# Two mixture-of-experts stages: expert slots padded to 128 rows in place of 256

## What is computed

```python
logits = einsum('tc,ec->te', x_flat, router_w)
probs = softmax(logits);  top_w, top_idx = top_k(probs, 2)
h = relu(einsum('tc,efc->tef', x_flat, w1) + b1)      # 8 experts, F = 1024
y = einsum('tef,ecf->tec', h, w2) + b2
out = sum over the 2 chosen experts of y * top_w      # layer 0
```

## Time and profile before

| | us |
|---|---|
| median of 3 runs (lowest, highest) | 1844.99 (1844.53, 1845.87) |
| the profiled execution | 1844.98 |
| its span, first to last instruction | 1843.3 |
| TensorE busy | 1593.0 (86%) |
| DVE, ACT, POOL busy | 1115.1, 853.1, 705.1 |
| mean granted TensorE clock | 0.922 |

### The profile page before, as it was taken

How to read it: one execution, slowest core, us unless ns; L and a number is a source line. 1 busy time by engine, 2 the same in 40 slices (tenths; PEclk the granted TensorE clock), 3 DMA queues, 4 the chain that set the end, 5 groups by cost and what they waited for, 6 DMA issues and landing times. The chain is left out here.

```text
span 1843.3 us, 38924 instructions
## 1 busy us (share of the span) xinstructions
PE 1593.0 (86%) x12460; PEld 1169.2 (63%) x12461; DVE 1115.1 (60%) x1945; ACT 853.1 (46%) x1518; POOL 705.1 (38%) x517
## 2 busy tenths in 40 slices
PE   4799798898897669999999996799988689999997
PEld 1433434434336658888888883577767568888886
DVE  4677687677687844555554441788876834444443
ACT  1664764755653425555554441376664322222221
POOL 2400401202200015555555442477771046555564
PEclk9999899899896589999999997699996789999999
DMA  4321311320414554555553222300005353333333
GB/s 132 100 79 46 114 55 36 114 68 23 138 35 168 187 206 92 137 137 137 137 137 69 46 41 38 92 25 17 8 24 180 106 149 59 59 62 60 57 60 44
DMA packets 104311, 159.85 MB, mean 87 GB/s; under 512 B 10810, under 2 KB 69998, under 8 KB 104110
## 3 DMA queue, kind: packets, MB, share of 16 engines
q1 hardware_dynamic: 73007, 117.52, 19.6%
q0 software_dynamic: 29952, 40.91, 12.6%
q10 hardware_dynamic: 1279, 0.46, 0.1%
HBM read 91.49 MB, written 67.37 MB: 86 GB/s over the span
## 5 line engine op out<-in xcount | busy, mean ns | idle before, releaser
L1249 PE MATMUL e_ph<-e_zTt,weights_a 128*128 128x256 f16 x3744 | 425.4, 274 | 29.3 <-issue 27.2
L1249 PEld LDWEIGHTS e_ph<-e_zTt,weights_a 128*128 x3744 | 360.9, 98 | 93.5 <-issue 49.8
L1203 POOL DMA_INDIRECT e_zt<-token_parts,slot_token x156 | 163.6, 1049 | 209.2 <-issue 198.4
L1382 DVE TENSOR_TENSOR e_hl<-e_h,e_hh 128x512 f16<-128x512 f32 x156 | 104.5, 691 | 228.4 <-ACT e_hh L1348 228.4
L1334 ACT ACTIVATE e_h<-e_ph,e_b 128x256 f32<-128x256 f32 x312 | 130.6, 470 | 232.8 <-PE e_ph L1249 155.8
L1213 POOL DMA_INDIRECT token_rows<-e_ysb,slot_token x78 | 148.2, 1901 | 206.9 <-DVE e_ysb L1399 192.5
L1263 PE MATMUL e_pyt<-weights_b,e_hh 128*128 x1248 | 210.7, 273 | 0.7 <-DVE e_ysb L1399 0.7
L647 ACT ACTIVATE probs<-lower_banks,shift 128x1024 f32<-128x1024 f32 x128 | 137.6, 1110 | 119.4 <-PE lower_banks L507 114.4
L1213 POOL DMA_INDIRECT out_dram<-e_ysb,slot_token x78 | 124.4, 1595 | 131.4 <-DVE e_ysb L1403 107.8
L1263 PE MATMUL e_pyt<-weights_b,e_hl 128*128 x624 | 170.2, 273 | 0.0
L1373 DVE SCALAR_TENSOR_TENSOR e_g<-e_ph,e_h 128x512 f32<-128x512 f32 x78 | 54.0, 692 | 174.1 <-PE e_ph L1249 174.1
(11 more groups left out here) (231 smaller groups left out, 2952.5 us busy)
## 6 DMA issues: line engine op xcount, KB each, us to landing
weight_parts<-w_split SPq DMA_DIRECT2D x32, 512.0 KB, 3.3
weights_a<-weight_parts SPq DMA_DIRECT2D x16, 1024.0 KB, 7.4
x_sb<-in_u SPq DMA_DIRECT2D x24, 512.0 KB, 5.1
weight_parts<-x_sb SPq DMA_DIRECT2D x24, 512.0 KB, 3.4
w_raw<-in_w1T SPq DMA_DIRECT2D x16, 512.0 KB, 4.4
w_raw<-in_w2T SPq DMA_DIRECT2D x16, 512.0 KB, 4.7
weights_b<-weight_parts SPq DMA_DIRECT2D x8, 1024.0 KB, 9.6
token_parts<-x_sb SPq DMA_DIRECT2D x8, 1024.0 KB, 5.3
```

The source lines that it names most:

```text
L1203: pool.indirect_dma_start(zt[:, i % 2, c, :], None, g.zrows, at).then_inc(ld[i % 2], 16)
L1249: last = pe.matmul(ph[:, q, f, :], up_w(wp, e, k, 2 * q + f), zTs[:, s, 2 * zp + k, :], start=(n == 0), stop=(n == 5))
L1382: dve.tensor_tensor(hl[:, s, 2 * q:2 * q + 2, :], src[:, q % 2], hh[:, s, 2 * q:2 * q + 2, :], ALU.subtract).then_inc(lo_done, 1)
```

## The change

A block of 128 slots is now the unit to which an expert's slots are padded. `BLOCKS` = 71 in place of 78. `PAIRS` = 28 tiles take two blocks of one expert, then 15 tiles take one block; `NT` = 43. An expert with an odd number of blocks has its last block among the single tiles. The slot numbering gets the steps for this: the ranks from `limit` on are moved `away` to the single tiles.

A single tile has the same number of matmuls in `up`, over 128 columns, and half of `turn` and `down`. It uses two banks of `ph`, by the tile's parity, with four groups of features in a bank where a double tile has two; `py` also goes by parity. In layer 0 a half of `up` is now four activations of 128 columns. Casts, subtractions and the gate product stay 512 columns wide, with one (layer 1) or two (layer 0) of each per single tile. Queues and their order stay; each engine's loop is split into one over double and one over single tiles, with the tiles between written out.

```diff
 C = 2
-NT = (2 * B * S + E * (C * P - 1)) // (C * P)
+BLOCKS = (2 * B * S + E * (P - 1)) // P
+PAIRS = (2 * B * S // P - E) // C
+NT = PAIRS + BLOCKS - C * PAIRS
...
-            step(dve.tensor_scalar(cnti[:], ptot[:, 0:E], float(C * P - 1), None, ALU.add))
-            step(dve.tensor_scalar(cntj[:], cnti[:], (C * P).bit_length() - 1, None, ALU.logical_shift_right))
-            step(dve.tensor_copy(cnt[:], cntj[:]))
-            step(dve.tensor_tensor_scan(cumt[:], g.ones[:, 0:E], cnt[:], 0.0, ALU.mult, ALU.add))
-            step(dve.tensor_tensor(base[:], cumt[:], cnt[:], ALU.subtract))
-            step(dve.tensor_scalar(base[:], base[:], float(C * P), None, ALU.mult))
-
-            step(dve.tensor_tensor(lg[:], prk[:, 0:T * E].rearrange("p (t e) -> p t e", e=E), over_t(base[:]), ALU.add))
+            step(dve.tensor_scalar(cnti[:], ptot[:, 0:E], float(P - 1), None, ALU.add))
+            step(dve.tensor_scalar(blocksi[:], cnti[:], P.bit_length() - 1, None, ALU.logical_shift_right))
+            step(dve.tensor_scalar(pairsi[:], blocksi[:], 1, None, ALU.logical_shift_right))
+            step(dve.tensor_scalar(oddi[:], blocksi[:], 1, None, ALU.bitwise_and))
...
+            step(dve.scalar_tensor_tensor(away[:], odd[:], float(P), away[:], ALU.mult, ALU.add))
+            ranks = prk[:, 0:T * E].rearrange("p (t e) -> p t e", e=E)
+            step(dve.tensor_tensor(wk2, ranks, over_t(limit[:]), ALU.is_ge))
+            step(dve.tensor_tensor(wk2, wk2, over_t(away[:]), ALU.mult))
+            step(dve.tensor_tensor(lg[:], ranks, over_t(base[:]), ALU.add))
+            step(dve.tensor_tensor(lg[:], lg[:], wk2, ALU.add))
...
+        def extent(i, single):
+
+
+            b = i + PAIRS if single else C * i
+            return b, 1 if single else C, 4 if single else 2
+
+        def place(x, single):
+
+            return x.rearrange("p (f t) -> p f t", f=4 if single else 2)
+
+        def landed(n, single):
+
+            return 16 * (n + PAIRS // 2) if single else 16 * C * n
...
             def add_rows(i):
 
                 s = i % 2
                 if i > 0:
-                    pool.wait_ge(sto[1 - s], 16 * C * ((i + 1) // 2))
-                for c in range(C):
-                    pool.wait_ge(yev, C * i + c + 1)
-                    at = bass.IndirectOffsetOnAxis(ap=g.slot_token[:, C * i + c:C * i + c + 1], axis=0)
+                    pool.wait_ge(sto[1 - s], landed((i - 1) // 2, i > PAIRS) + 16 * (1 if i > PAIRS else C))
+                b, cols, _ = extent(i, i >= PAIRS)
+                for c in range(cols):
+                    pool.wait_ge(yev, b + c + 1)
+                    at = bass.IndirectOffsetOnAxis(ap=g.slot_token[:, b + c:b + c + 1], axis=0)
...
-                for q in range(Q):
+                for q in range(UB * cols):
+                    bank = 2 * s + q if single else q
...
-                                last = pe.matmul(ph[:, q, f, :], up_w(wp, e, k, 2 * q + f), zTs[:, s, 2 * zp + k, :],
+                                last = pe.matmul(out[:, f, :], up_w(wp, e, k, per * q + f), zTs[:, s, 2 * zp + k, 0:cols * P],
...
-                for c in range(C):
+                for c in range(cols):
                     if not early:
-                        hold(pe, g, yev, C * i - C + c + 1)
+                        hold(pe, g, yev, b + c - 1)
                     n = 0
                     for f in range(NF):
                         for wp, hp in ((0, hh), (0, hl), (1, hh)):
-                            last = pe.matmul(py[c][:, 0, :], hp[:, s, f, c * P:(c + 1) * P], down_w(wp, e, f),
+                            last = pe.matmul(py[s if single else c][:, 0, :], hp[:, s, f, c * P:(c + 1) * P], down_w(wp, e, f),
...
+            loop(1, LOOP1, False)
+            unrolled(2 * LOOP1, 2 * LOOP2[0])
+            loop(*LOOP2, True)
+            unrolled(2 * LOOP2[1], NT)
...
-                        for f in range(2):
-                            last = act.activation(h32[:, q % 2, f, :], ph[:, q, f, :], ACT.Relu,
-                                                  bias=b1[:, bass.ds(e, 1), 2 * q + f], scale=1.0 / WS)
+                        for f in range(per):
+                            last = act.activation(place(h32[:, slot], single)[:, f, :], place(ph[:, bank], single)[:, f, :],
+                                                  ACT.Relu, bias=b1[:, bass.ds(e, 1), per * q + f], scale=1.0 / WS)
...
-                dve.tensor_copy(zTs[:, s], pz[s][:]).then_inc(zev, 1)
+                dve.tensor_copy(zTs[:, s, :, 0:cols * P], pz[s][:, :, 0:cols * P]).then_inc(zev, 1)
```

More of the change, by code:

```diff
@@ L1266, in down, with loop, unrolled @@
                     last.then_inc(dn_done, 1)
+            def loop(first, last, single):
+                with pe.Fori(first, last) as n:
+                    _, e = nc.values_load_multi_w_load_instructions(g.expert[0:1, bass.ds(2 * n, 3)], engines=[mybir.EngineType.PE],
+                                                                    min_val=0, max_val=E - 1)
+                    for s in range(2):
+                        i = 2 * n + s
+                        up(i + 1, 1 - s, e[s + 1], False, single)
+                        turn(i + 2, s, n + 1, False, single)
+                        down(i, s, e[s], False, single)
+            def unrolled(first, last):
+                e = [expert_of(pe, i) for i in range(first, min(last + 1, NT))]
+                for i in range(first, last):
+                    if i + 1 < NT:
+                        up(i + 1, (i + 1) % 2, e[i + 1 - first], False, i + 1 >= PAIRS)
+                    if i + 2 < NT:
+                        turn(i + 2, i % 2, i // 2 + 1, False, i + 2 >= PAIRS)
+                    down(i, i % 2, e[i - first], False, i >= PAIRS)
             e = [expert_of(pe, i) for i in range(3)]
@@ L1336, in units @@
                     else:
-                        last = act.activation(h32[:, q], ph[:, q], ACT.Silu, scale=1.0 / WS)
+                        last = act.activation(h32[:, slot], ph[:, bank], ACT.Silu, scale=1.0 / WS)
                     last.then_inc(act_done, 1)
                 def high(q):
+                    slot = s if layer and single else q % 2
                     if layer == 0:
-                        act.wait_ge(act_done, HQ * i + q + 1)
+                        act.wait_ge(act_done, HB * b + q + 1)
@@ L1385, in result @@
-            def result(i, s, half, early):
+                for q in range(HB * cols):
+                    slot = s if layer and single else q % 2
+                    dve.wait_ge(hi_done, HB * b + q + 1)
+                    dve.tensor_tensor(hl[:, s, per * q:per * q + per, 0:cols * P], place(src[:, slot], single),
+                                      hh[:, s, per * q:per * q + per, 0:cols * P], ALU.subtract).then_inc(lo_done, 1)
+            def result(i, s, half, early, single=False):
+                b, cols, _ = extent(i, single)
@@ L1419, in weight_low, with loop @@
                                          ALU.mult, ALU.subtract).then_inc(w_lo, 1)
-            for first, last in ((1, SPLIT), (SPLIT, TAIL // 2)):
+            def loop(first, last, single, with_weights):
                 with dve.Fori(first, last) as n:
@@ L1424, in _, with unrolled @@
                         i = 2 * n + s
[L1425 to L1428 removed]
+                        hidden(i + 1, 1 - s, False, single)
+                        evacuate(i + 2, s, False, single)
+                        result(i, s, n, False, single)
+                        if with_weights:
                             weight_low(n, s)
[L1430 to L1436 removed]
+            def unrolled(first, last):
+                for i in range(first, last):
+                    if i + 1 < NT:
+                        hidden(i + 1, (i + 1) % 2, False, i + 1 >= PAIRS)
+                    if i + 2 < NT:
+                        evacuate(i + 2, i % 2, False, i + 2 >= PAIRS)
+                    result(i, i % 2, i // 2, False, i >= PAIRS)
+            for first, last in ((1, SPLIT), (SPLIT, LOOP1)):
+                if first < last:
+                    loop(first, last, False, layer == 0 and first == 1)
+            unrolled(2 * LOOP1, 2 * LOOP2[0])
+            loop(*LOOP2, True, False)
+            unrolled(2 * LOOP2[1], NT)
+            dve.wait_ge(yev, BLOCKS)
 def attention1_context(nc, g, a, at):
```

226 lines of the change are left out of this document (117 added, 109 removed).

## The result

Before 1845.24 us, after 1872.98 us (medians of four runs of each on one chip); ratio 1.0151, interval 1.0130 to 1.0172. The change makes the kernel 28 us slower, where the forecast had it 49 us faster. The profiled execution after took 1876.91 us, span 1875.0.

What follows compares the result with a forecast made beforehand. TensorE's matmuls bound the kernel before; single tiles would wait for DVE's copy. First stage -33.0, second -20.8, routing +4.4 sum to -49.4 us, from 1844.98 to 1795.6; range 1776 to 1816.

Steps and rivals of the forecast that it cites:

- Matmuls of a single tile: Both expert stages: `up` keeps 48 matmuls and lasts 2.86 us, `turn` 0.22, `down` 2.62 and 1.31.
- I take 0.056: Single tiles' `up`: 0.056 us between 128-column matmuls, read from fp16 transposes with a fresh weight load each.
- The bounds of this cost: Spacing of matmuls in single tiles' `up`: between 0.056 us and 0.109, the latter no gain from fewer columns.
- the slower ones: Rivals on weight loads in `up`: 0.083 us a matmul, +38, 1834, chance 0.06; 0.109, +76, 1872, chance 0.05.
- the far end: Rival: weight loads bind `up` wholly at 0.109 us a matmul, +76 us, 1872, slower than before; chance 0.05.
- its +36 us: Single tiles' `up` at the Trainium skill's 81 ns a matmul: 36 us more than the forecast sum.
- The loop's 0.72 us falls into this wait and costs nothing: Second stage's single tiles: TensorE's turn of the loop lies within the wait for DVE's copy and adds nothing.
- The wait for DVE's copy: Single tiles' `up` waits for product, cast, subtraction, copy: 5.3 us a tile second stage, 6.4 first; rival 1778, 0.10.
- ACT: First stage: four 128-wide activations for each half of `up`, 0.31 us each; rival 0.42, +12, 1808, chance 0.10.
- POOL: Single tiles' scatters, 3.99 us start to start, and gathers cost nothing; rival that scatters bind, 1818, chance 0.07.
- Routing: DVE's slot numbering: more steps, smaller one-hot operations; +2.2 us a layer, +4.4 for both, bounds +1 and +4 each.
- The stage sums: Expert stages with their ends: first stage -33.0 us, second stage -20.8 us.

Runs made afterwards that it cites:

- experiment one: The kernel after, with `up` of single tiles reading expert 0's weights at a fixed address: 1817.18 us, ratio to before 0.9836.
- seven: The kernel after, with a fixed address only for the weights' low part in `up` of single tiles: 1823.19 us, ratio to before 0.9883.
- eight: The kernel after, with the third of each three matmuls in single tiles' `up` reading the weights' high part again: 1828.17 us, ratio to before 0.9896.
- the control, six: The kernel before, with its `up` reading expert 0's weights at a fixed address: 1839.62 us, ratio to before 0.9971.
- the fourth kernel: The kernel after, with DVE's copy before the subtractions and TensorE's single tiles written out four at a time: 1845.82 us, ratio to before 1.0000.
- Experiments two to four: The kernel after with DVE's copy first in single tiles, 1858.33 us; with TensorE's single tiles written out, 1867.88; with both, 1845.82.
- experiment five: The kernel after, with single tiles' `up` at a fixed weight address, DVE's copy first and TensorE's single tiles written out: 1804.69 us, ratio to before 0.9787.

## Why the prediction was wrong

**Matmuls of a single tile: this step failed.** "I take 0.056" came from transposes with fixed addresses. In `up` of a single tile two register instructions for three matmuls hold TensorE's queue, and at a granted clock of 1.00 the 48 last 4.27 us, (4.27 - 0.22) / 47 = 0.086 apart. Experiments one, seven and eight show the cause, and the control, six, why nothing of it was to be seen before. On the 30 single tiles it costs 56 us: 30 x (4.4 - 2.86) = 46 in the `up`s themselves (4.4 as their usual length in the rows), and about 10 around them, most of it at the ten turns of the loop, where the gap behind the copy is 1.5 us with register addresses and 0.6 without. The two expert stages are 71.5 us over the forecast: these 56, and 15.5 that the first experiment has too.

The bounds of this cost were right, 0.056 and 0.109, and gave the slower ones 0.06 and 0.05. Their mechanism, weight loads, is refuted: loads of 95 to 98 ns stand 0.056 apart in experiment one. Even so their prices came near: 1872 for the far end, where 1873 was measured, partly by chance, as 0.109 was not reached and the loop made up for it. The row that would have warned me was in the trace of before: 32 register instructions of 46 ns in each `up`. Against a spacing of 0.109 they looked idle; I never asked what they would be against 0.056.

The Trainium skill (TensorE: Matmul & The Clock Gate, Back-to-back issue gap) gives about 81 ns for a matmul of 128 columns in a stream with loads, and its +36 us was nearer to the result than my sum. As a rule of loads and matmuls alone, though, the trace does not agree with it: with fixed addresses 48 pairs in a row keep 0.056 us.

**"The loop's 0.72 us falls into this wait and costs nothing": failed too.** It supposed that TensorE's queue turns the loop while the engine waits for the copy. The gap stands behind the copy: 1.56 - 0.13 = 1.43 us at a turn of the second stage, 1.46 - 0.35 = 1.11 in the first, about 12 us over the ten turns. With fixed addresses it is 0.2 to 0.7 (once 2.0), so a good part of it is again the registers' doing, and already in the 56 us. Before, the turn showed as 0.72 behind 24 matmuls and 0.73 behind 48: it did not depend on the length of `down` there. What covers queue work seems to be the lead that the queue has over the engine. That such a lead exists, and that it shortens an `up`, the profile after shows in one `up` of a single tile behind the 48 matmuls of a double tile's `down`, with the same register addresses and a clock of 1.00 (the records from 1004.3 us on):

```profile
1004.38 2.99 PE L1297 MATMUL e_ph<-e_zTt,weights_a 128*128 128x128 f16 x48
L1297 PEldq FUSED_REGOPS  x21: 46/46/46, 1004.3 to 1007.0; - x21
```

Eleven of its 32 register instructions had run before its first matmul, and it takes 2.99 us. In the fourth kernel `up`s without a gap in front, at a clock of 1.00, take 3.28 us with 24 left, 4.02 with 29, and 4.3 to 4.5 with all 32. The usual single tile after starts with all 32. That it has no lead left to cover the turn with is argued from this, not shown by an experiment. Experiments two to four show that the turn and the wait for the copy stand in for one another: either alone gives little. A turn is a branch and the loading of three numbers; no run gives the branch a price of its own.

**Left out: the loads between the loops.** Where the loop over double tiles ends, five expert numbers are loaded one by one in front of the `up` of tile 27, and TensorE idles for 1.98 and 1.81 us there, in the first and the second stage. The sum had nothing for it. In the first experiment, which has it too, `up` of tile 29 starts 1.8 and 1.6 us later in its stage than forecast.

**The wait for DVE's copy: held.** From the start of the product to that of the copy 1792.24 - 1790.19 = 2.05 us, forecast 1.99; the copy 0.42, forecast 0.38; the start of `up` 0.13, forecast 0.06 (0.35 in the first stage). With the registers out of the way a period is 5.4 us without the turn (forecast 5.3), and in the first stage 6.5 (6.4).

**ACT: held.** Four activations of 128 columns in 1.14 us, under the 4 x 0.31 I had:

```profile
1048.64 1.14 ACT L1400 ACTIVATE e_h<-e_ph,e_b 128x128 f32<-128x128 f32 x4 [3.76 <-PE e_ph L1297]
```

**POOL: held in this kernel.** 3.75 us from a scatter to its landing; POOL waits for a landing at the end of each stage, 2.4 us, and once more, for 1.19 us, at 1762. Where all else is taken away (experiment five) it is next: in the second stage every second scatter waits for a landing, the last three start 4.2 us apart, and `turn` waits for gathers.

**Routing: held, within its bounds.** DVE's timeline after:

```profile
623.87 0.17 DVE L1063 TENSOR_SCALAR e_ei<-e_ptot 128x8 int32<-128x8 f32 x1 [1.21 <-PE e_ptot L931]
...
626.59 0.42 DVE L1078 TENSOR_TENSOR e_lane_hot<-e_prk,e_e 128x256 f32<-128x256 f32 x1
...
656.74 0.16 DVE L1122 TENSOR_SCALAR e_cum<-e_cum 128x8 f32<-128x8 f32 x1
...
660.31 0.23 DVE L1133 TENSOR_TENSOR slot_token<-e_pinv,e_spare 128x71 uint32<-128x71 f32 x1
```

13 small steps in 2.72 us and the ten behind the one-hot blocks in 3.57 (forecast 3.5). The first gather comes 1.8 to 4.2 us later in the kernels with this routing, against 2.2. Between the stages the table has 4.3 to 8.1 us more, but the control, whose routing is that of before, also has 3.9 more there, in a stretch of attention where the granted clock differs from run to run (1131 to 1475 us: 0.83 before, 0.80 after, 0.82 in the control). What of it is the change's stays open. The last 1.7 to 1.9 us of "rest" I had not costed.

**The stage sums** were too low even at the price that they assumed. The first experiment has that price and the forecast's order on every queue, and its stages take 439.4 and 346.7 us against 433.2 and 337.4. Of these 15.5 us about 3.4 are the loads between the loops, 6 the ten turns, and 1.3 an `up` that ran in part at half the clock; the rest is not split. That experiment five comes near the forecast (434.2 and 340.0) is luck: there the copy is not waited for, and loads and POOL take its place.

## What to carry to other kernels

A price per instruction is taken from a row that has the same operands, not just the same shape: an address from a register brings instructions of its own into the engine's queue, and halving the width of a matmul halves their cover. When work is made shorter, go through everything that is hidden beside it today, queue instructions and turns of loops included, and ask of each what it costs against the new length. And a gap that the profile calls "issue" does not melt into another wait on the same queue unless a run shows it.

## What the runs showed of the hardware that I had not expected

- Register instructions on TensorE's queue are recorded at 46 ns, but two of them per three 128-column matmuls stretch three matmuls from 0.168 to 0.26 us or more, and one per three costs nothing. If each matmul's own share of the queue is i and a register instruction's r, then 3i + 2r is about 0.26 and 3i + r at most 0.168: r is at least 0.09 us, twice its record (an estimate from these runs).
- Loading one expert number on TensorE's queue leaves 0.53 us open behind a `down` of 12 matmuls, 0.2 or less behind one of 24; each further number costs 0.41 us in one call for many, 0.67 by single calls.
- The granted clock fell from 1.00 to 0.50 among the single tiles, for 3.4 us (twice 6.8), where TensorE was waiting or had just waited, for 1.6 to 5.6 us; in the profile after, 5 waits of 1.8 to 2.2 us were followed by a fall and 7 of 1.6 to 2.3 were not, and in the kernel that loads one number per tile, without such waits, it never fell there. With a fall an `up` with 16 register instructions takes up to 4.48 us in place of 2.85, but one with 32 mostly 4.4 to 5.0 in place of 4.3 to 4.5, which fits a queue that holds it at either clock.
